# Two table stages of a two-layer graph kernel: all groups' gathered rows are projected first, the destinations' rows behind them, and VectorE normalises four groups of the second stage

## The reference, cut to what matters

```python
h = jnp.maximum(_layernorm(x), 0.0)              # 6250 nodes x 128
xl = h @ Wl + bl;  xr = h @ Wr + br              # layer 1, graph attention
m = leaky_relu(xl[src] + xr[dst] + edge_attr @ We)        # 106250 edges, sorted by dst
...                                              # softmax over each dst, weighted sum of xl[src]
x = x + batchnorm(gelu(h + attention))
h = jnp.maximum(_layernorm(x), 0.0)
em = concatenate([h[src], h[dst]]) @ msg_w + msg_b        # layer 2, messages
em = relu(layer_norm(em)) * edge_weights
messages = segment_sum(em, dst) / counts
gate = sigmoid(h @ gate_w + gate_b)
h_new = relu(layer_norm(concatenate([h, messages]) @ upd_w + upd_b))
x = x + gate * h_new + (1 - gate) * h
```

## Time and profile before

| | us |
|---|---|
| median of 3 runs (2269.47 to 2271.11) | 2270.16 |
| the profiled execution | 2270.79 |
| its span in the profile | 2269.0 |
| busy in it: PE 1644.5, DVE 1709.5, ACT 1232.5, POOL 1634.4 | |
| POOL's gathers from `src_table` (x1638, L643), busy | 1564.7 |

### The profile page before, as it was taken

One profiled execution on the slowest core, in us unless ns is written; L12 is line 12 of the kernel. 1 busy time (PEld: TensorE's weight loads), 2 busy tenths in 40 slices (PEclk: granted clock), 3 DMA queues, 4 the chain that ended last, 5 costly groups with the idle time before them and its releaser, 6 DMA issues.

```text
span 2269.0 us, 43295 instructions
## 1 busy us (share of the span) xinstructions
PE 1644.5 (72%) x9256; PEld 1231.5 (54%) x9256; DVE 1709.5 (75%) x6093; ACT 1232.5 (54%) x3996; POOL 1634.4 (72%) x1742
## 2 busy tenths in 40 slices
PE   5488887777778777877776767767766776666666
PEld 4265555555545555555565555555655655555454
DVE  6787777676777777777768777778778778777777
ACT  5344444444434444444556666667666666566655
POOL 5777777777777777777137777777777777777774
PEclk9799999999999999999978888888888888898988
DMA  9433333333333333332242332332333333323322
GB/s 190 100 86 86 86 78 84 86 77 84 78 86 77 82 81 84 77 83 72 54 114 66 85 83 78 84 84 76 83 84 76 83 85 80 79 76 83 76 68 62
DMA packets 176752, 189.19 MB, mean 83 GB/s; under 512 B 100940, under 2 KB 132708, under 8 KB 176564
## 3 DMA queue, kind: packets, MB, share of 16 engines
q0 software_dynamic: 54192, 111.40, 20.0%
q1 hardware_dynamic: 120965, 75.89, 13.1%
q10 hardware_dynamic: 1472, 0.73, 0.2%
HBM read 172.91 MB, written 14.97 MB: 83 GB/s over the span
## 4 chain that ended last, share of the span: by engine, by line
POOL 31%; issue 18%; PE 14%; DVE 12%; ACT 10%; DMA 3%; DVEq 2%; POOLq 1%; ACTq 0%
POOL room L643 31%; PE psum L888 4%; ACT room L1206 4%; PE psum L892 3%; DVE room L1818 3%; DMA room<-src_table,rec 3%; ACT room L1209 2%; PE psum L815 2%; ACT rows L1186 2%; ACT room L1198 1%; PE psum L715 1%; PE psum L797 1%; DVE room L1804 1%; DVEq L1535 1%; DVE dfar L1561 1%
## 5 line engine op out<-in xcount | busy, mean ns | idle before, releaser
L643 POOL DMA_INDIRECT room<-src_table,rec x1638 | 1564.7, 955 | 519.1 <-issue 482.1
L888 PE MATMUL psum<-room,ident 128*128 128x384 f32 (+1 forms) x512 | 286.0, 645 | 295.7 <-ACT room L1209 207.0
L1186 ACT ACTIVATE rows<-psum 128x128 f32<-128x128 f32 x832 | 216.9, 271 | 318.3 <-DVE room L1804 318.3
L892 PEld LDWEIGHTS psum<-room 125*128 125x128 f32 x1664 | 277.0, 230 | 112.5 <-issue 64.1
L815 PE MATMUL psum<-room 128*125 128x128 f32 x1664 | 255.9, 294 | 85.8 <-ACT room L1136 81.9
L1118 ACT ACTIVATE room<-psum 128x384 f32<-128x384 f32 (+1 forms) x256 | 130.4, 509 | 289.6 <-PE psum L787 281.6
L815 PEld LDWEIGHTS psum<-room 128*125 128x125 f32 x1664 | 210.3, 195 | 136.6 <-ACT room L1136 135.5
L1599 DVE TENSOR_TENSOR room<-psum,room 128x384 f32<-128x384 f32 (+1 forms) x256 | 150.9, 590 | 173.4 <-ACT room L1118 88.5
L892 PE MATMUL psum<-room 125*128 125x128 f32 x1664 | 273.4, 312 | 0.0
L888 PEld LDWEIGHTS psum<-room,ident 128*128 128x128 f32 x512 | 92.1, 225 | 315.2 <-ACT room L1209 167.0
L1804 DVE TENSOR_TENSOR room<-psum,msg_g 128x384 f32<-128x384 f32 (+1 forms) x256 | 150.2, 587 | 149.9 <-PE psum L892 149.9
(11 more groups left out here) (250 smaller groups left out, 2650.6 us busy)
## 6 DMA issues: line engine op xcount, KB each, us to landing
room<-dst_perm SPq DMA_DIRECT2D x128, 416.0 KB
room<-src_table,rec POOLq DMA_INDIRECT x1638
src_table<-rows SPq DMA_DIRECT2D x24, 224.0 KB
node_x<-in_x SPq DMA_DIRECT2D x5, 560.0 KB
x_rows<-node_x SPq DMA_DIRECT2D x12, 224.0 KB
out_rows<-node_x SPq DMA_DIRECT2D x12, 224.0 KB
rec<-rec_rows SPq DMA_DIRECT2D x125, 19.5 KB
pair_info<-pair_list SPq DMA_DIRECT2D x128, 2.0 KB
```

The costliest lines, as they stand in the source:

```text
L643: pool.indirect_dma_start(out=xg[:, u, t * P:(t + 1) * P], out_offset=None, in_=table[:, :], in_offset=bass.IndirectOffsetOnAxis(ap=rec[:, ...
L888: nc.tensor.matmul(msg_bank[b][:, cols], ident[:, :], xg[:, u, t0 * P:t1 * P], start=True, stop=False, skip_group_check=True)
L892: i = nc.tensor.matmul(msg_bank[b][:, j * P:(j + 1) * P], msg_oht[0:W, v, t * P:(t + 1) * P], dwin[0:W, v, :], start=False, stop=(t == t1 ...
L1186: i = nc.scalar.activation(sq[:, j * P:(j + 1) * P], msg_bank[b][:, j * P:(j + 1) * P], ACT.Square, accum_out=var_e[:, c, j:j + 1])
```

## The change

`project` now multiplies by the first half of the weights only, into one PSUM bank of four instead of a pair of two, so PE may run four groups ahead of DVE, and `add_bias` makes only the add into `rows`. The second halves are projected by a new PE function `project_near` after all 13 groups, and their bias is added by a new DVE function `near_rows`. On DVE this stands behind `raw_scale`. In layer 2 DVE normalises groups 9 to 12 (14 tiles, without the relu, which `features` makes anyhow) ahead of its adds, and ACT leaves these out. `update_own` waits for all of `near_rows`.

```diff
+        half_ps = [banks[2 + u].rearrange("p (i f) -> p i f", i=GT) for u in range(4)]
+        NORM_DVE = (9, 10, 11, 12)
         def turn_rows(pe, n, g):
             t0, t1 = GROUPS[g]
-            pe.wait_ge(s_norm, n * NGX + g + 1)
+            if n == 1 and g in NORM_DVE:
+                pe.wait_ge(s_norm_dve, NORM_DVE.index(g) + 1)
+            else:
+                pe.wait_ge(s_norm, n * NGX + g + 1)
...
         def project(pe, n, g, weights):
-            ge(pe, s_row, n * NGX + g - 1 if g > 1 else 0)
+            ge(pe, s_row, n * NGX + g - 3 if g > 3 else 0)
+            if n == 1 and g < 4:
+                pe.wait_ge(s_near_row, NG)
             for t in range(t0, t1):
-                i = nc.tensor.matmul(rows_ps[g % 2][0:PP, t - t0, :], feat_h[:, t, :], weights[:, :], start=True, stop=True)
+                i = nc.tensor.matmul(half_ps[g % 4][0:PP, t - t0, :], feat_h[:, t, :], weights[:, 0:D], start=True, stop=True)
             i.then_inc(s_proj, 1)
+
+        def project_near(pe, n, g, weights):
+            t0, t1 = GROUPS[g]
+            if g < 4:
+                pe.wait_ge(s_row, n * NGX + NG + g - 3)
+            else:
+                pe.wait_ge(s_near_row, n * NG + g - 3)
+            for t in range(t0, t1):
+                i = nc.tensor.matmul(half_ps[(NG + g) % 4][0:PP, t - t0, :], feat_h[:, t, :], weights[:, D:2 * D], start=True, stop=True)
+            i.then_inc(s_near_proj, 1)
...
+            for g in range(NG):
+                project_near(pe, n, g, weights)
...
             def update_own(g):
-                pe.wait_ge(s_row, NGX + NG)
+                pe.wait_ge(s_near_row, 2 * NG)
...
-                    if ahead <= g + 2 < NG:
+                    if ahead <= g + 2 < NG and (n == 0 or g + 2 not in NORM_DVE):
                         norm_rows(n, g + 2)
...
-                for h, to in enumerate((rows[0:PP, g % 3, 0:nt, :], dst_rows[:, t0:t1, :])):
-                    f = slice(h * D, (h + 1) * D)
-                    i = dve.tensor_tensor(to, rows_ps[g % 2][0:PP, 0:nt, f],
-                                          bias[0:PP, f].unsqueeze(1).to_broadcast([PP, nt, D]), ALU.add)
-                i.then_inc(s_row, 1)
+                dve.tensor_tensor(rows[0:PP, g % 3, 0:nt, :], half_ps[g % 4][0:PP, 0:nt, :],
+                                  bias[0:PP, 0:D].unsqueeze(1).to_broadcast([PP, nt, D]), ALU.add).then_inc(s_row, 1)
+
+            def near_rows(n, bias):
+                for g, (t0, t1) in enumerate(GROUPS):
+                    nt = t1 - t0
+                    dve.wait_ge(s_near_proj, n * NG + g + 1)
+                    dve.tensor_tensor(dst_rows[:, t0:t1, :], half_ps[(NG + g) % 4][0:PP, 0:nt, :],
+                                      bias[0:PP, D:2 * D].unsqueeze(1).to_broadcast([PP, nt, D]), ALU.add).then_inc(s_near_row, 1)
...
             raw_scale(0, gat)
+            near_rows(0, b_lr)
             rest_of_weights(0)
...
             layer_norm_scale(1, 1)
+            dve.wait_ge(s_norm_scale, PART0[1] + 2)
+            for g in NORM_DVE:
+                for t in range(*GROUPS[g]):
+                    i = dve.tensor_scalar(node_h[:, t, :], node_x[:, t, :], rstd[:, t:t + 1], nmr[:, t:t + 1], ALU.mult, ALU.add)
+                i.then_inc(s_norm_dve, 1)
             tables(1, msg_b, {})
             raw_scale(1, msg)
+            near_rows(1, msg_b)
```

More of the change, by code:

```diff
@@ L281, in gnn_layers @@
         s_row = sem("s_row")
+        s_near_proj = sem("s_near_proj")
+        s_near_row = sem("s_near_row")
+        s_norm_dve = sem("s_norm_dve")
+        NORM_DVE = (9, 10, 11, 12)
         s_src_out = [sem(f"s_src_out{u}") for u in range(3)]
@@ L744, in raw_turn @@
             t0, t1 = BLK[b]
-            pe.wait_ge(s_norm, raw_group(n, b) + 1)
+            pe.wait_ge(s_norm, raw_group(n, b) + 1 - (len(NORM_DVE) if n == 1 else 0))
             for t in range(t0, t1):
```

## The result

The changed kernel takes 2280.38 us (median, 2275.82 to 2282.98), the kernel before in the same runs 2270.57 (2269.47 to 2271.15): a ratio of 1.0039, with a 95% interval of 1.0029 to 1.0049 (the two medians divided give 1.0043). It is 9.8 us slower. The forecast was 2277.5, with 0.58 for slower.

What follows compares the result with a forecast made beforehand. POOL's gather pace was taken as the bound, with each layer's end set by POOL's last late start. Layer 1 +6.7 and layer 2 +0.6 gave +7.3 on 2270.79, 2278.1; the median, 0.6 below, 2277.5 us; range 2268.5 to 2283.0.

Steps and rivals of the forecast that it cites:

- Which limit decides each layer: Both layers: an earlier table gains at most POOL's later margins (1.3 and 3.5 us); a later loop start costs the excess.
- the two kinds of POOL waits: POOL waits 6 to 11 us before layer 1's pair 4 for the sum, some 8 us in layer 2 for records.
- Rival (b): Both layers: the earlier table counts in full, -3.5 - 7.1 = -10.6 us, 2259.6 us; chance 0.13.
- The margin is about 1.3 us: Layer 1: pair 0's first sum ends at 113.64, pair 4's first gather, needing it, starts at 115.02.
- 54.8, not 57.8: Layer 1's first pass: the last add into `rows` ends at 54.8 us instead of 57.8, with fewer adds on DVE.
- the store's 4.2 us: Layer 1's first pass: 4.2 us from an add's end to its landed store, taken between 3.2 and 4.7.
- the forecast 3.5: Layer 1: the table is stored at 59.0, so POOL could start 3.5 us earlier.
- Layer 1's second pass, 11.0: `near_rows` runs from 59.3 to 70.3: 9.0 us at full clock plus 2 for the slow clock.
- The 2 us for the clock: Layer 1's second pass: after PE stands still, half-speed work for some 4 us loses 2 us.
- Layer 2's clock: Layer 2's second pass: PE restarts after 4 us idle and loses the same 2 us; `near_rows` ends at 1186.1, not 1184.1.
- Layer 2's sum: Layer 2: loop start +4.1 us, less pair 5's record margin of 3.5, so the layer ends 0.6 us later.
- VectorE's normalising "at nothing": Layer 2's first pass: DVE's 14 normalising instructions take 3.8 us, fit its 3.74 us of idling and cost nothing.

Runs made afterwards that it cites:

- the centring: Changed kernel with VectorE's centring of layer 2's weights moved from ahead of layer 1's loop to that loop's end: 2277.03 us.
- the early records: Layer 2's records issued once pair k - 1's gathers landed, not after its messages: 2272.47 us on the changed kernel, 2263.34 with layer 1's stage as before.
- the last kernel of the table: Kernel before with only layer 2's table stage changed, and layer 2's records issued after pair k - 1's gathers landed: 2263.34 us, ratio 0.9970.
- the kernels of the table: Kernel before (2270.26 us), changed kernel (2280.38) and its variants: each stage alone, centring late, PE kept busy, earlier records; 2263.34 to 2278.77 us.
- the changed kernel with early records: Changed kernel, with layer 2's records issued once pair k - 1's gathers landed instead of after its messages: 2272.47 us, ratio 1.0007.
- one with the old stage: Kernel before with only layer 1's table stage changed, layer 2's stage as before: 2278.77 us, ratio 1.0036.

## Why the prediction was right, and where its sizes were off

**Which limit decides each layer: right.** The margins were read as small in layer 1 and somewhat larger in layer 2, so an earlier table would be lost and a later loop paid for. That is what the two kinds of POOL waits, the centring and the early records show. Rival (b), the earlier table in full, needed the records moved: it holds for layer 2 in the last kernel of the table.

**"The margin is about 1.3 us" (layer 1): too large.** It counted to the end of the sum. The gather starts 0.79 us behind that end (123.06 + 1.14 = 124.20, then 124.99), so the margin was 0.6: +10.6 at the loop's start gave +10.0 at pair 4.

**Layer 1's first pass (the adds into `rows`), "54.8, not 57.8": mis-sized.** The last add ended at 57.2, and between 56.3 and 57.0 in other runs of this stage. (Its own terms, 50.1 + 4.2 + 0.4, give 54.7.) The term is the store's 4.2 us, above all in front of the tenth add, which was forecast at 49.5 without a wait:

```profile
41.96 0.69 DVE L1341 TENSOR_TENSOR rows<-psum,b_lr 125x512 f32<-125x512 f32 x1 [1.46 <-DMA src_table<-rows]
...
51.52 1.47 DVE L1341 TENSOR_TENSOR rows<-psum,b_lr 125x512 f32<-125x512 f32 x2 [1.41 <-DMA src_table<-rows]
```

The tenth add uses the slot of the seventh, which ended at 42.65. By the profile's releaser that store landed only before 51.52, 8.9 us later, and this is 2.0 of the 2.4 us. The last add in turn waited 4.6 us from the tenth's end, not 4.2. In the other runs of this stage the tenth add comes at 51.0 to 51.4. The last store landed faster than forecast (60.36 - 57.21 = 3.2), so POOL still got 2.1 us of the forecast 3.5; DVE reached `near_rows` 2.0 us later than forecast.

**Layer 1's second pass, 11.0: 11.9 here and 10.6 in others.** The 9.0 at the full clock is exactly what layer 2 shows. The 2 us for the clock was a good mean of 1.6 to 2.9.

**Layer 2's clock: wrong.** The forecast charged the same 2 us behind an idle time of 4 us; PE idled 2.81 us and kept the full clock. Over the kernels of the table the second passes sort by the idle time of PE in front of them. Behind 2.58 to 2.90 us (five passes, all in layer 2) the 68 projections took 7.69 us. Behind 3.28, 3.65, 3.67 and 3.70 us (layer 1) they took 9.36, 9.36, 10.63 and 9.35, at half the clock in part. In the changed kernel with early records, layer 2's pass stood behind 3.16 us and took 9.36, with a granted clock of 0.50 in 1185 to 1187, though its first pass was as dense as the others'. So a dense first pass doesn't keep the clock by itself; whether layer 1's sparser one helps to lose it no run shows. What failed is the forecast's 4 us of idling: PE's four groups ahead ended 2.0 us behind the last add into `rows` (1183.20 and 1181.16), not 1.0. The section that the forecast cited (the Trainium skill, TensorE: Matmul & The Clock Gate, HAM oscillation) speaks of long waits between bursts, and the rows on the longer waits agree with it.

**Layer 2's sum: 2.1 too large.** Beside the clock, the first pass ended earlier too (the last add ended 21.6 us behind the layer's first gather, 22.7 forecast). The loop started 72.3 us behind that gather, 71.3 before: +0.9, not +4.1. Pair 5's records were issued at 1258.27 and its gather started 2.9 us on, where the forecast had 2.1 for the landing; so the margin of pair 5 was 2.7 us and not 3.5. Even so that gather stood 101.6 us behind the layer's first, 102.6 before, and the layer came out 1.5 us shorter, not 0.6 longer. In the profiles of the other kernels with this stage it is 1.2, 0.7 and 0.2 shorter, and 0.4 in one with the old stage, so the gain is of the order of 1 us and hardly beyond scatter.

**VectorE's normalising "at nothing": right in size and place.** 14 instructions, 3.68 us (3.8 forecast), and the first add came at 1163.13, 3.5 us behind the layer's first gather, where it was 3.7 before.

```profile
1159.53 3.68 DVE L1780 TENSOR_SCALAR node_h<-node_x,rstd,nmr 125x128 f32<-125x128 f32 x14
```

**Not in the forecast: the hand-over, +1.6 us.** No step of the change touches it (see the last section). The sum by parts: 6.7 forecast and 10.0 measured, 0 and 1.6, 0.6 and -1.5; in all 7.3 and 10.1 at the last gather. Layer 1 was sized 3.3 us too small and the hand-over left out, layer 2 was sized 2.1 too large; that the errors went against each other is luck.

## What to carry to other kernels

Where a producer with few buffers sets the pace, a table stored earlier is worth only the margin of the next thing that the producer waits for: list its waits one by one (table, records, buffer) with their margins before moving work, because each one you remove shows the next. Work taken out of a pass in front is not gone; if it lands ahead of the consumer's start on an in-order engine it costs in full, and if PE stood still before it, it may run at half the clock as well. Here the change is worth keeping in layer 2 alone, and with the records issued earlier: 2263.34 us, 0.3% faster than before. How much of this the earlier records would bring by themselves is open.

## What the runs showed of the hardware

The granted clock differs between executions of the same code. PE's lines between the layers, before (1105 to 1150 us) and after (1115 to 1160), by the view of groups (count, busy us, mean ns, idle before and its releasers):

```profile
L861 PE MATMUL psum<-ident,feat_room 128*125 128x128 f32 x50 | 12.9, 413 | 8.8 <-ACT feat_room L1174 5.7 <-DVE node_x L1732 2.9
L852 PE MATMUL psum<-ident,feat_room 125*128 125x125 f32 x50 | 8.1, 282 | 2.7 <-DVE feat_room L1694 2.4
L848 PE MATMUL psum<-ident,node_h 125*128 125x125 f32 x50 | 7.6, 274 | 2.0 <-DVEq L1655 2.0
```

```profile
L883 PE MATMUL psum<-ident,feat_room 128*125 128x128 f32 x50 | 14.3, 447 | 7.5 <-ACT feat_room L1196 4.1 <-DVE node_x L1760 3.2
L874 PE MATMUL psum<-ident,feat_room 125*128 125x125 f32 x50 | 9.5, 319 | 2.1 <-DVE feat_room L1722 1.9
L870 PE MATMUL psum<-ident,node_h 125*128 125x125 f32 x50 | 9.0, 308 | 2.0 <-DVEq L1683 2.0
```

The same 150 operations take 28.6 us of PE before and 32.8 after, with a granted clock of 1.00 in the first 5 us (1104 to 1109) before and 0.50 after (1116 to 1121). From the last gather of layer 1 to the first of layer 2 it is 57.5 us before and 59.2 after. In the other kernels of the table the two go together: 29.6 us of PE with 58.3, 31.6 to 31.7 with 58.2 to 58.3 (three kernels), 32.8 with 59.0 and 59.1 (two). That the hand-over's 1.6 us come from the clock is supported by this, but no run changed it on purpose. And on two of the chips the kernel before took 2994.85 and 3016.86 us, a third more than on the others, with all engines stopping together. What stops them the profile doesn't say beyond the word "remote", and it stays open.
